# Linear attention in a fused two-layer kernel: the norm factor of the outputs applied behind the output projection, on VectorE, with the order of TensorE, VectorE and ScalarE in a step laid out anew

## The reference

```
# S: state per value head; o: output per token
o = einsum('bhkv,bhk->bhv', S, q_t)
og = o * silu(z)
og = og * rsqrt(mean(og * og, axis=-1) + EPS) * norm_weight   # per token and value head, over 128
return og.reshape(Bv, Tv, VDIM) @ W_out                         # sums over the 32 value heads
```

## Time and profile before

| | |
|---|---|
| median of 3 runs | 1351.96 us (1344.74 to 1357.4) |
| the profiled execution | 1348.03 us, of it 1346.0 us span from first to last instruction |
| busy share | PE 89%, DVE 69%, ACT 62%, POOL 55% |
| mean granted clock of TensorE | 0.948 of full speed |

### The profile page before, as it was taken

How to read it: one execution, slowest core, us unless ns; L and a number is a source line. 1 busy time by engine, 2 the same in 40 slices (tenths; PEclk the granted TensorE clock), 3 DMA queues, 4 the chain that set the end, 5 groups by cost and what they waited for, 6 DMA issues and landing times. The chain is left out here.

```text
span 1346.0 us, 30471 instructions
## 1 busy us (share of the span) xinstructions
PE 1203.4 (89%) x10744; PEld 1019.1 (76%) x10744; DVE 924.2 (69%) x2304; ACT 829.4 (62%) x2289; POOL 744.7 (55%) x1187
## 2 busy tenths in 40 slices
PE   7888998999999999999999999999998787997886
PEld 6787787787878888878877888878877676765654
DVE  6886877787878787887778787878772423325663
ACT  6335666666667676766666767667675535217773
POOL 2285756667676758585857667676757301112201
PEclk9776999999999999999999999999997869999997
DMA  4214041413121222214040403121123120001000
GB/s 168 74 38 106 6 104 7 105 24 87 31 80 35 75 41 71 53 58 103 7 107 5 106 20 91 27 83 36 36 41 108 30 94 1 0 27 41 2 9 24
DMA packets 143430, 72.82 MB, mean 54 GB/s; under 512 B 116744, under 2 KB 132624, under 8 KB 141360
## 3 DMA queue, kind: packets, MB, share of 16 engines
q1 hardware_dynamic: 143280, 70.89, 20.7%
HBM read 57.06 MB, written 13.78 MB: 53 GB/s over the span
## 5 line engine op out<-in xcount | busy, mean ns | idle before, releaser
L1011 POOL TENSOR_TENSOR tmp<-Dm,Tn 64x31 f32<-64x31 f32 (+15 forms) x496 | 262.4, 529 | 89.4 <-DMA Dm<-blk_in_scratch 54.1
L1014 POOL TENSOR_TENSOR Tn<-Tn,tmp 64x31 f32<-64x31 f32 (+15 forms) x496 | 285.4, 575 | 38.9
L823 DVE SCALAR_TENSOR_TENSOR cv<-bank,cw,cv 128x255 f32<-128x255 f32 (+2 forms) x384 | 155.2, 474 | 78.0 <-ACT cv L629 78.0
L987 POOL TENSOR_TENSOR ro<-ss,mhalf 128x4 f32<-128x4 f32 x64 | 65.1, 1017 | 250.1 <-ACT junk L691 214.0
L823 DVE SCALAR_TENSOR_TENSOR cqk<-bank,cw,cqk 128x255 f32<-128x255 f32 (+2 forms) x384 | 154.9, 473 | 7.5 <-ACT cqk L629 7.5
L454 PE MATMUL bank<-wo,OTs 128*128 128x256 f32 x512 | 138.6, 405 | 10.8 <-ACT OTs L722 10.8
L883 DVE SCALAR_TENSOR_TENSOR BP<-bank,cj,E 128x512 f32<-128x512 f32 (+1 forms) x256 | 142.8, 611 | 2.7 <-DVE cj L868 0.5
L691 ACT ACTIVATE junk<-og 128x129 f32<-128x129 f32 x256 | 79.9, 312 | 97.3 <-issue 80.6
L887 DVE TENSOR_TENSOR R<-Vs,bank 128x256 f32<-128x256 f32 x64 | 27.0, 421 | 141.9 <-PE bank L420 138.3
L454 PEld LDWEIGHTS bank<-wo,OTs 128*128 128x128 f32 x512 | 93.1, 197 | 25.8 <-ACT OTs L722 14.2
L699 ACT ACTIVATE ogn<-og,ro 128x128 f32<-128x128 f32 x256 | 81.9, 398 | 29.5 <-POOL ro L987 29.5
(11 more groups left out here) (210 smaller groups left out, 3492.7 us busy)
## 6 DMA issues: line engine op xcount, KB each, us to landing
rvz<-in_L_attn_W_qkvz SPq DMA_DIRECT2D x16, 512.0 KB, 5.0
x<-alpha_scratch SPq DMA_DIRECT2D x8, 1024.0 KB, 6.4
alb<-alpha_scratch SPq DMA_DIRECT2D x7, 1024.0 KB, 6.4
rqk<-in_L_attn_W_qkvz SPq DMA_DIRECT2D x16, 256.0 KB, 2.6
wo<-in_L_attn_W_out SPq DMA_DIRECT2D x16, 256.0 KB
blk_in_scratch<-BP SPq DMA_DIRECT2D x256, 16.0 KB, 1.5
tinv_scratch<-Tn SPq DMA_DIRECT2D x32, 128.0 KB, 2.1
tinv_t_scratch<-Tt SPq DMA_DIRECT2D x32, 128.0 KB, 2.2
```

Of the source, the lines that this page charges most:

```text
L823: nc.vector.scalar_tensor_tensor(d, bk[:, t * T:(t + 1) * T - s], cw[p][:, first + t, TAPS - 1 - s:TAPS - s], d, ALU.mult, ALU.add).then_i ...
L1011: pool_step_done(nc.gpsimd.tensor_tensor(t, Dm[:, j, j + 1:BLK].unsqueeze(2).broadcast_to([SLOTS, r, c]), Tn[:, j, 0:c].unsqueeze(1).broad ...
L1014: pool_step_done(nc.gpsimd.tensor_tensor(Tn[:, j + 1:BLK, 0:c], Tn[:, j + 1:BLK, 0:c], t, ALU.subtract), kh * NTS + 2 * j + 4)
```

## The change

The factor ro of a token and value head no longer scales og before it is turned. `act_ogn` and its buffer ogn are gone; `pe_ot` turns og itself. Since ro differs between the two value heads, the projection can't sum over them in PSUM: `pe_f` writes each head's product apart (one chunk fills the whole bank), and `dve_acc` sums them into acc with two scalar_tensor_tensor instructions for each chunk, times ro, the second waiting for the first. So `pe_f` of chunk 1 waits for `dve_acc` of chunk 0. The streams are laid out anew round this:

- TensorE: `pe_ot` stands first behind the q/k projection (b = 2, 3) or behind merge stage 0 (b = 0, 1). In steps 2 and 3, `pe_f` of chunk 0 stands behind solve0, ahead of `pe_vt`, `pe_v` and solve1; chunk 1 ahead of solve2. In steps 0 and 1, `pe_vt` moves between merge stages 2 and 3, chunk 1 of `pe_f` between solve1 and solve2.
- ScalarE: `act_ots` stands behind tap 0 of q/k (b = 2, 3) or behind merge stage 0; in steps 0 and 1 `act_vs` moves up ahead of the split and merge stage 3.
- VectorE: in steps 2 and 3 `dve_acc` of chunk 0 stands ahead of `dve_r2`, chunk 1 between the taps of q/k and those of v; in steps 0 and 1 chunk 0 ahead of `dve_r2` and chunk 1 behind it.

```diff
             def pe_ot(kh, p, b, scaled):
-                wait(nc.tensor, "ogn", at(kh, b, 4, 4))
+                wait(nc.tensor, "og", at(kh, b, 2, 2))
                 wait(nc.tensor, "vs", min(scaled, 2 * NG))
                 for h in range(R):
                     for c in range(NC):
                         n = h * NC + c
-                        last = nc.tensor.transpose(bOT[:, n * P:(n + 1) * P], ogn[:, c, h, :], ident)
+                        last = nc.tensor.transpose(bOT[:, n * P:(n + 1) * P], og[b % 2][:, c, h, 0:DK], ident)
                 last.then_inc(sem("ot"), 1)
             def pe_f(kh, p, b, c):
+
                 if c == 0:
                     wait(nc.tensor, "ots", at(kh, b, 1, 1))
-                    wait(nc.tensor, "acc", at(kh, b, 1))
                     if b == 0:
                         wait(nc.tensor, "wo_in", (kh + 1) * 16)
+                wait(nc.tensor, "acc", at(kh, b, 4, 2 * c))
                 for h in range(R):
-                    last = nc.tensor.matmul(bF[:, c * D:(c + 1) * D], OTs[:, h, c, :], wo[p][:, h, :],
-                                            start=(h == 0), stop=(h == R - 1))
-                if c == 1:
-                    last.then_inc(sem("f"), 1)
+                    last = nc.tensor.matmul(bF[:, h * D:(h + 1) * D], OTs[:, h, c, :], wo[p][:, h, :], start=True, stop=True)
+                last.then_inc(sem("f"), 1)
...
@@ -575,17 +573,17 @@
                     if vz:
                         pe_v(*vz, 0)
                     pe_merge(kh, p, b, 0)
+                    if last:
+                        pe_ot(*last, 2 * (now + 2))
                     if vz:
                         pe_v(*vz, 1)
                     pe_before_ot(kh, b)
-                    if last:
-                        pe_ot(*last, 2 * (now + 2))
                     pe_merge(kh, p, b, 1)
                     if last:
                         pe_f(*last, 0)
                     pe_merge(kh, p, b, 2)
-                    if last:
-                        pe_f(*last, 1)
+                    if vt:
+                        pe_vt(*vt, now)
                     pe_merge(kh, p, b, 3)
                     if vz:
                         pe_z(*vz, 0)
@@ -593,30 +591,30 @@
                     if vz:
                         pe_z(*vz, 1)
                     pe_solve(kh, p, b, 1)
-                    if vt:
-                        pe_vt(*vt, now)
+                    if last:
+                        pe_f(*last, 1)
                     pe_solve(kh, p, b, 2)
                     pe_o(kh, p, b, 0)
                     pe_o(kh, p, b, 1)
                 else:
+                    pe_ot(*last, 2 * (now + 2))
                     pe_solve(kh, p, b, 0)
                     pe_behind_solve(kh, b)
+                    pe_f(*last, 0)
                     if vt:
-                        pe_vt(*vt, now - 1)
+                        pe_vt(*vt, now)
                     if vz:
                         pe_v(*vz, 0)
                     pe_solve(kh, p, b, 1)
                     if vz:
                         pe_v(*vz, 1)
                     pe_before_ot(kh, b)
-                    pe_ot(*last, 2 * (now + 3))
+                    pe_f(*last, 1)
                     pe_solve(kh, p, b, 2)
                     pe_o(kh, p, b, 0)
                     pe_o(kh, p, b, 1)
                     if kh == NKH - 1 and b == B - 1:
                         pe_turn_w1(12, 3)
-                    pe_f(*last, 0)
-                    pe_f(*last, 1)
                     if vz:
                         pe_z(*vz, 0)
...
-            def act_ogn(kh, p, b):
-                wait(nc.scalar, "ro", at(kh, b, 1, 1))
-                wait(nc.scalar, "ot", at(kh, b, 1))
-                for c in range(NC):
-                    for h in range(R):
-                        n = c * R + h
-                        nc.scalar.activation(ogn[:, c, h, :], og[b % 2][:, c, h, 0:DK], ACT.Copy, scale=ro[b % 2][:, n:n + 1]).then_inc(sem("ogn"), 1)
...
             def act_ots(kh, p, b):
                 wait(nc.scalar, "ot", at(kh, b, 1, 1))
-                wait(nc.scalar, "f", at(kh, b, 1))
+                wait(nc.scalar, "f", at(kh, b, 2))
...
@@ -768,18 +758,18 @@
                 if qk:
                     act_tap0(*qk, "qk", bQK, cqk, 0)
                 if merges(b):
+                    act_merge(kh, p, b, 0)
                     if last:
-                        act_ogn(*last)
-                    act_merge(kh, p, b, 0)
+                        act_ots(*last)
                     if vz:
                         act_tap0(*vz, "v", bV, cv, 2)
                     act_before_ots(kh, b)
-                    if last:
-                        act_ots(*last)
                     act_merge(kh, p, b, 1)
                     if vz:
                         act_silu_v(*vz)
                     act_merge(kh, p, b, 2)
+                    if vt:
+                        act_vs(*vt)
                     splits(kh, p, b, act_split_qk, act_split_vz)
                     act_merge(kh, p, b, 3)
                     if qk:
@@ -788,18 +778,15 @@
                     if vz:
                         act_silu_z(*vz)
                     act_y(kh, p, b, 1)
-                    if vt:
-                        act_vs(*vt)
                 else:
+                    act_ots(*last)
                     act_y(kh, p, b, 0)
                     if vt:
                         act_vs(*vt)
-                    act_ogn(*last)
                     act_before_ots(kh, b)
                     if vz:
                         act_tap0(*vz, "v", bV, cv, 2)
                     act_y(kh, p, b, 1)
-                    act_ots(*last)
...
-            def dve_acc(kh, p, b):
-                wait(nc.vector, "f", at(kh, b, 1, 1))
-                a = acc[:, NC * b:NC * (b + 1), :].rearrange("p c d -> p (c d)")
-                wait(nc.vector, "acc", at(kh, b, 1, 1 - B))
-                nc.vector.tensor_tensor(a, a, bF[:], ALU.add).then_inc(sem("acc"), 1)
+            def dve_acc(kh, p, b, c):
+                wait(nc.vector, "f", at(kh, b, 2, c + 1))
+                wait(nc.vector, "ro", at(kh, b, 1, 1))
+                a = acc[:, NC * b + c, :]
+                for h in range(R):
+                    wait(nc.vector, "acc", at(kh, b, 4, c * R + h))
+                    nc.vector.scalar_tensor_tensor(a, bF[:, h * D:(h + 1) * D], ro[b % 2][:, c * R + h:c * R + h + 1], a,
+                                                   ALU.mult, ALU.add).then_inc(sem("acc"), 1)
...
@@ -926,16 +917,21 @@
                     dve_scales(*gram)
                     dve_bp(*gram, 0)
                 if not merges(b):
+                    dve_acc(*last, 0)
                     dve_r2(kh, p, b)
                 if gram:
                     dve_bp(*gram, 1)
                 for taps in (taps_v, taps_qk) if merges(b) else (taps_qk, taps_v):
                     for n in range(1, TAPS):
                         taps(n)
-                if last:
-                    dve_acc(*last)
+                    if taps is taps_qk and not merges(b):
+                        dve_acc(*last, 1)
                 if merges(b):
+                    if last:
+                        dve_acc(*last, 0)
                     dve_r2(kh, p, b)
+                    if last:
+                        dve_acc(*last, 1)
                 else:
                     dve_og(kh, p, b)
...
             def pool_ro(kh, p, b):
                 wait(nc.gpsimd, "ss", at(kh, b, 4, 4))
-                wait(nc.gpsimd, "ogn", at(kh, b, 4, -4))
+                wait(nc.gpsimd, "acc", at(kh, b, 4, -4))
...
@@ -1311,11 +1307,10 @@
                 for m in range(2):
                     pe_gate_up(0, m)
                 pe_ot(NKH - 1, 1, B - 1, 2 * NG)
-                pe_gate_up(0, 2)
-                for c in range(NC):
-                    pe_f(NKH - 1, 1, B - 1, c)
-                for m in range(3, HT):
+                for m in range(2, HT):
                     pe_gate_up(0, m)
+                    if m < 4:
+                        pe_f(NKH - 1, 1, B - 1, m - 2)
...
                 for m in range(3):
                     dve_hact(0, m)
-                dve_acc(NKH - 1, 1, B - 1)
+                dve_acc(NKH - 1, 1, B - 1, 0)
                 ln_norm(dve, 1, 2)
+                dve_acc(NKH - 1, 1, B - 1, 1)
```

More of the change, by code:

```diff
@@ L248, in build @@
             og = [sb(f"og{i}", [P, NC, R, DK + 1], ctx=s1) for i in range(2)]
-            ogn = sb("ogn", [P, NC, R, DK], ctx=s1)
             junk = sb("junk", [P, DK + 1], ctx=s1)
@@ L973, in dve_behind @@
                     nc.vector.wait_ge(sem(f"x_in{b - 1}"), 32)
[L974 removed]
+                    nc.vector.wait_ge(sem("acc"), at(NKH - 1, b, 4))
                     residual(ch, rt[:], b - 1, acc[:, NC * (b - 1):NC * b, :], 0, 0, "res0a")
@@ L1052, in sp_load_wo @@
             def sp_load_wo(kh):
-                wait(nc.sync, "f", at(kh - 1, 0, 1))
+                wait(nc.sync, "f", at(kh - 1, 0, 2))
```

7 lines of the change are left out of this document (3 added, 4 removed).

## The result

The changed kernel takes **1510.43 us** (median of 4 runs, 1505.73 to 1521.5) against 1349.78 us of the kernel before beside it (4 runs, 1344.74 to 1357.4): ratio 1.1197, 95% interval 1.1114 to 1.1279. The profiled execution has a span of 1509.0 us; TensorE's mean granted clock is 0.903 in it (0.948 before).

The account below looks back on a forecast made before the run. The prediction took TensorE as pace-setter, with VectorE's chain from solve1 to z nearly level in steps 2 and 3. Profiled 1348 + 112 (chains) + 56 (clock) = 1516, forecast 1520 us since the profile lies 4 below the median; range 1440 to 1580.

Parts of the forecast that it names:

- last heads: Key heads 14 and 15, without q/k taps, 8 steps: 6 us of waiting for ogn goes, bounds 0 and 11.
- What bounds the kernel: Regular steps: TensorE sets the pace; in steps 2 and 3 VectorE's chain from solve1 to z runs nearly level.
- The pair: Two chained sums of 256 columns on VectorE: 0.93 us, bounds 0.8 to 1.1; 1.3 us more a step.
- The chain from solve1 to z: VectorE's work behind solve1 in steps 2 and 3: from 6.69 us to 7.6 with the pair between the taps.
- Steps 2 and 3: +4.2 us to 18.0 and +2.6 us to 16.4, with TensorE idle 3.5 us ahead of z.
- The waits for OTs: TensorE ahead of projection 0: about 0.8 us in step 3 and 1.6 us in step 2.
- Steps 0 and 1: Vs ahead of merge stage 3's evacuation delays solve1: +1.15 us in step 0, +0.6 in step 1, bounds 0 and 1.5.
- The clock: Idle time ahead of z drops TensorE to half clock: 28 falls at 2.0 us each, +56 us.
- Rival 1: Only the chains lengthen and the clock holds: 1464 us, chance 0.25.
- rival 3: Clock stays low longer, lengthened by step 2's idle time ahead of projection 0: 1597 us, chance 0.10.
- The sum: Chains 95 + 8 + 15 - 6 = +112 us, clock +56 us.
- Rival 4: VectorE has room, and TensorE runs on without its waits for ogn: 1309 us, chance 0.04.

Follow-up runs that it names:

- thin1: Changed kernel with the pair of sums between the q/k and v taps cut to one column in steps 2 and 3 (output incomplete): 1492.21 us, ratio 1.1049.
- thin0: Changed kernel with the pair of sums ahead of R2 cut to one column in steps 2 and 3 (output incomplete): 1510.16 us, ratio 1.1195.
- pool_split: Kernel before, with rows 25 to 30 of the 32x32 inverses on POOL moved from step 2 to step 3: 1333.79 us, ratio 0.9922.
- fill: Changed kernel with eighteen unused matmuls ahead of z in steps 2 and 3 of key heads 0 to 13: 1457.75 us, ratio 1.0805.
- f_behind: Changed kernel; in steps 2 and 3 projection 0 back behind solve1, projection 1 behind the outputs, first pair behind R2 and Gram factors: 1530.38 us, ratio 1.1345.
- ot_behind: Changed kernel; in steps 2 and 3 turn of og, OTs, projection 0 and first pair behind solve1, projection 1 behind the outputs: 1507.45 us, ratio 1.1218.
- vt_back: Changed kernel; in steps 0 and 1 the turn of v back behind projection 1 and Vs at the end of ScalarE's step: 1525.23 us, ratio 1.1344.
- relaid: Kernel before with the change's arithmetic in another order, both pairs behind all taps, projection 1 between z's halves in steps 2 and 3: 1358.25 us, ratio 1.0126.
- bp_late: Kernel before, with the second pair of Gram factors on VectorE moved behind the taps in steps 2 and 3: 1402.07 us, ratio 1.0426.
- best: Kernel before, with second Gram factors behind the taps in steps 2 and 3 and new shares of POOL's inverses for each step: 1382.43 us, ratio 1.0311.

## Why the prediction was right

1510 us stand against 1520 forecast, and the steps of the argument mostly hold. That the sum comes so near is partly luck: the clock cost more in the regular steps than was forecast, and gave back in the last heads what was not forecast at all.

*What bounds the kernel.* "It has no slack behind solve1; VectorE's idle time lies ahead of R2": right, and tested from both sides. thin1 (behind) moves the time, thin0 (ahead) doesn't. pool_split shows it from the side of the kernel before: the removed wait was for the most part covered by VectorE's chain.

*The pair.* Its row shows 1.00 us (0.99 between the taps) where 0.93 was taken, within its bounds; one sum takes 0.50 where og of the same width takes 0.42. On the chain it costs 0.91 us, from its start at 564.50 to the start of the taps of v at 565.41. The chain from solve1 to z came to 7.48 us where 7.6 was forecast; the missing 0.1 lies ahead of R, which starts 0.64 us behind solve1 and not 0.75.

*Steps 2 and 3.* The waits for OTs are 0.62 and 1.66 us, forecast 0.8 and 1.6. At the full clock, in fill, step 3 takes 16.43 (forecast 16.4) and step 2 takes 18.2 (forecast 18.0). solve1 of step 3 stands at t = 8.8 in the changed kernel, whose step begins at half clock, and at 7.4 in fill (forecast 7.2). z waits 3.2 us where 3.5 was forecast. f_behind and ot_behind show that this is not the fault of one instruction: the wait for OTs, the bank that OTs shares with the turn of v, and the pairs ahead of the taps each hold z late by themselves.

*Steps 0 and 1.* At the full clock both cost less than their terms: 18.3 in fill against 17.5 is +0.8 for step 0, forecast +1.15; 17.9 to 18.2 against 18.1 is about nothing for step 1, forecast +0.6. Both lie within the bounds given for them. The reason given for step 0 (Vs ahead of the evacuation) wasn't separated: vt_back moves it back and uncovers another wait.

*The clock.* The trace shows half clock at each of the 28 late z, and taking the idle time away by filling gives back 53 us; the price set was 56. Rival 1, that the clock holds, falls by this. What the forecast left out are the other 16 stretches. The six behind a wait of 1.66 us for OTs in step 2 are a part of rival 3, which expected them in all 14 steps 2; the ten between the merge stages stood in no term and no rival. The Trainium skill, "TensorE: Matmul & The Clock Gate", section "HAM oscillation — how this bites in real kernels", describes just this pattern, a stall repeated in each round with each round starting at half clock; the 28 waits of 3.2 us, each with a stretch at 0.50, agree with it.

*The sum.* For the 55 steps the forecast has 95 + 8 + 15 = 118 us of chains and 56 of clock, together 174, and 186.6 were measured. Two accounts divide the 186.6. By TensorE's time, 111.9 are idle time and 74.7 busy time for the same passes. By fill, the chains at the full clock take 70.6 to 71.2 us a head against 63.2, times 13.75 heads 102 to 110 us, which leaves 77 to 85 for the clock. So the chains were taken 6 to 16 us too high, and the clock 19 to 29 us too low. This largest miss was offset by the last heads, where -6 stood and 22.3 us went.

All of that gain lies in the last two key heads (139.99 - 116.72 = 23.3 us), and what follows them is 1.0 us longer (209.71 against 208.74). Of the 23.3 us only 5.0 are idle time, near the 6 that the forecast let go. The other 18.3 are TensorE's busy time (114.60 - 96.35), at a clock of 0.96 in place of 0.80: the long waits for ogn, with the half clock behind them, are gone. The forecast gave this no term. So idle time rose by 111.9 - 5.0 = 107 us in all where 112 was forecast, and busy time by 74.7 - 18.3 = 56 where 56 was set for the clock. The second agreement is chance: 28 falls at z were priced, and what was paid is 44 stretches less those that went from the last heads.

*The other side.* Rival 4, room on VectorE, needed the chain from solve1 to z to fit under 4.1 us of work on TensorE; it is 7.48. In relaid, where both pairs stand behind the taps and off that chain, the arithmetic still doesn't pay: ratio 1.0126, and 29 us in the regular steps.

## What to carry to other kernels

When a wait is to be removed, measure the chain that ends next on the same instruction: here a wait of 1.54 us was worth 0.48, because another chain ended almost level. New work belongs in the gap of an engine and not merely on the engine with idle time: the pair ahead of the handover from solve1 to R was free (thin0), the pair behind it was paid (thin1). A wait on TensorE is to be priced with the clock behind it: in bp_late and best, most of the loss was dense work at half clock and not the waiting. Before an instruction is deferred, follow its result through every in-order queue up to the last reader, the DMA issuer's included: four of the moves above (f_behind, ot_behind, bp_late, best) failed on a shared bank or an in-order queue that their plan left out.
